# Staging of weight casts, two moved weight loads and a last loop without GpSimd arithmetic, in an eight-core Trainium2 kernel

## The reference

```python
xn = layernorm(x)
mixed_q = xn @ Wq + bq ; mixed_k = xn @ Wk + bk
q_w = softmax((mixed_q @ Wqa + bqa) / 8, over the rows)      # 16 heads
pooled_q = sum over rows of q_w * mixed_q                     # one vector of 1024
mixed_qk = mixed_k * pooled_q
k_w = softmax((mixed_qk @ Wka + bka) / 8, over the rows)
pooled_k = sum over rows of k_w * mixed_qk
s = (pooled_k * mixed_q) @ Wt + bt + mixed_q
y = relu(xn @ W_fc.T)**2 @ W_proj.T                           # hidden width 4096
spikes = five steps of a threshold recurrence on y, their mean
out = x + s * silu(spikes)
```

## Time and profile before

| what | us |
|---|---|
| the timed runs | 1747.59 and 1940.24, median 1843.92 |
| the profiled execution | 1742.46 |
| its span on the slowest core (core 7) | 1740.9 |
| spans of the 8 cores | 1725.4 to 1740.9 |
| TensorE matmul busy | 1333.2 (77% of the span) |
| DVE, ACT, POOL busy | 706.6, 382.5, 228.6 |

### The profile page before, as it was taken

The page is one execution under the profiler, slowest core; times in us unless marked ns, Lnnn a source line. Parts: engine busy times, 40 slices in busy tenths (PEclk is TensorE's granted clock), DMA queues, the critical chain, the costliest instruction groups (busy, mean ns, idle before and its releaser), DMA issues.

```text
span 1740.9 us, 26823 instructions; the slowest of 8 cores (1725.4 to 1740.9 us)
## 1 busy us (share of the span) xinstructions
PE 1333.2 (77%) x8997; PEld 833.0 (48%) x8997; DVE 706.6 (41%) x1297; ACT 382.5 (22%) x828; POOL 228.6 (13%) x308
## 2 busy tenths in 40 slices
PE   0001999999999999999999999999931460558884
PEld 0000666666666666666666666666620130223332
DVE  3222435545546455465464553653432211322221
ACT  1332221322313213223122132231210101021111
POOL 1332000000000000000000000000000102035454
PEclk9999999999999999999999999999965755779997
DMA  5996101111011011110110111101075219147774
GB/s 162 290 295 210 62 13 62 43 44 55 32 62 56 20 61 43 44 56 31 62 56 25 56 43 44 44 25 43 26 225 165 84 30 297 55 137 232 224 230 162
DMA packets 59648, 170.00 MB, mean 98 GB/s; under 512 B 9415, under 2 KB 9815, under 8 KB 59498
## 3 DMA queue, kind: packets, MB, share of 16 engines
q1 hardware_dynamic: 34810, 86.29, 16.8%
q0 software_dynamic: 24704, 82.00, 13.5%
HBM read 117.80 MB, written 50.46 MB: 97 GB/s over the span
## 4 chain that ended last, share of the span: by engine, by line
PE 67%; DMA 15%; DVE 6%; ACT 4%; issue 4%; POOL 2%; SPq 2%; DVEq 0%; ACTq 0%; POOLq 0%
PE PS L481 26%; PE PS L460 24%; PE PS L375 6%; DMA AM<-cnt_scratch 3%; DMA OB<-WfcT 3%; DMA OB<-WprojT 3%; PE PS L854 3%; PE PS L625 2%; POOL OB L883 2%; PE PS L379 2%; DVE YS L877 2%; PE PS L760 2%; DMA OB<-Wk 1%; ACT YS L490 1%; DMA AB<-xn_scratch 1%
## 5 line engine op out<-in xcount | busy, mean ns | idle before, releaser
L481 PE MATMUL PS<-AB,AM 128*128 128x512 bf16 x2048 | 533.5, 380 | 15.5 <-ACT YS L490 13.8
L460 PE MATMUL PS<-SCA,AB 128*128 128x256 bf16 x4096 | 530.3, 273 | 0.0
L460 PEld LDWEIGHTS PS<-SCA,AB 128*128 128x128 bf16 x4096 | 400.5, 98 | 153.2
L469 DVE TENSOR_TENSOR AM<-RB 128x256 bf16<-128x256 f32 x512 | 217.1, 424 | 481.5 <-PE PS L481 283.3
L465 ACT ACTIVATE RB<-PS 128x256 f32<-128x256 f32 x512 | 196.7, 384 | 793.6 <-PE PS L460 327.9
L481 PEld LDWEIGHTS PS<-AB,AM 128*128 128x128 bf16 x2048 | 186.6, 98 | 172.6 <-issue 31.4
L375 PE MATMUL PS<-SCA,AM 128*128 128x256 bf16 x1024 | 137.2, 277 | 139.7 <-DVE SCA L383 116.9
L375 PEld LDWEIGHTS PS<-SCA,AM 128*128 128x128 bf16 x1024 | 100.6, 99 | 155.5 <-issue 142.9
L515 DVE SCALAR_TENSOR_TENSOR AM<-YS,AM 128x1024 bf16<-128x1024 f32 x128 | 156.0, 1219 | 0.8
L854 PE MATMUL PS<-AM,AB 128*128 128x512 bf16 x384 | 95.1, 397 | 37.0 <-issue 21.7
L519 POOL DMA_DIRECT2D cnt_scratch<-AM x32 | 20.6, 645 | 756.2 <-DVE AM L469 419.6
(11 more groups left out here) (107 smaller groups left out, 773.7 us busy)
## 6 DMA issues: line engine op xcount, KB each, us to landing
XF<-x SPq DMA_DIRECT2D x64, 512.0 KB, 4.5
out<-OB POOLq DMA_DIRECT2D x32, 512.0 KB, 6.3
xn_scratch<-SCA POOLq DMA_DIRECT2D x16, 512.0 KB, 3.6
xtm_scratch<-SCA POOLq DMA_DIRECT2D x32, 256.0 KB, 4.9
OB<-WfcT POOLq DMA_DIRECT2D x32, 256.0 KB, 6.3
YS<-WfcT SPq DMA_DIRECT2D x32, 256.0 KB, 6.5
YS<-WprojT SPq DMA_DIRECT2D x32, 256.0 KB, 5.6
OB<-WprojT POOLq DMA_DIRECT2D x32, 256.0 KB, 5.6
```

The lines of the kernel that those rows point to most:

```text
L460: pl.comp("tensor", lambda te, hb=hb, lt=lt, rh=rh, c=c: te.matmul(hb[:, 0:256], lt, rh, start=(c == 0), stop=(c == 7)), reads=a1keys(c * ...
L469: pl.comp("vector", lambda v, h2=h2, rr=rr: v.tensor_mul(h2, rr, rr), reads=[krr], writes=[("h2", g3)])
L481: pl.comp("tensor", lambda te, yb=yb, lt=lt, rh=rh, j=j: te.matmul(yb[:], lt, rh, start=(j == 0), stop=(j == 31)), reads=[kh2] + a2keys(j ...
```

## The change

1. `cast_nslots` starts at 4 and is never set to 8. The slots 2 and 6 of the list, used in the four-slot rotation, are now loaded by SyncE's queue (they hold ACT's pieces); 0 and 4 stay with GpSimd. All staging lies in OB.
2. The small casts of Wqa and Wka move from the end of startup to just behind Wq.
3. The load of the q scores is issued before the 32+12 loads of the transition, hence before the barrier. Three groups of `patch_total` go.
4. 16 pieces of Wt are cast into AM right behind those of WkT. The casts of Wt behind the pooling of k stay as well, so Wt is loaded and cast twice.
5. Wk is cast into AB2[24576:32768] and read from there. The mixed_q blocks 8 to 11 that lay there are loaded behind the pooling of k.
6. All 16 loads of mixed_q go from SyncE's queue to GpSimd's: 8 ahead of the Wk casts, 8 behind the pooling of k and ahead of the Wt casts.
7. Last loop: silu into two buffers of YS in turn, the DVE products straight into OB, and the add of x as a DVE instruction in place on OB. GpSimd only issues the stores.

```diff
-            ("gpsimd", "lw4", OB[:, 512:1024], ("stg", 0)),
-            ("sync", "lw5", YS[:, 512:1024], ("ys", 0)),
+            ("sync", "lw5", OB[:, 512:1024], ("stg", 0)),
+            ("gpsimd", "lw4", YS[:, 512:1024], ("ys", 0)),
...
-            ("gpsimd", "lw6", OB[:, 1536:2048], ("stg", 1)),
-            ("sync", "lw7", YS[:, 1536:2048], ("ys", 1)),
+            ("sync", "lw7", OB[:, 1536:2048], ("stg", 1)),
+            ("gpsimd", "lw6", YS[:, 1536:2048], ("ys", 1)),
-        cast_nslots = [8]
+        cast_nslots = [4]
...
-            for wsrc, dst, nm in ((Wqa_d, WA, "WA"), (Wka_d, WB, "WB")):
...
             cast_flush()
-            cast_nslots[0] = 4
-
-        cast_nslots[0] = 8
         for d in range(8):
             cast(Wq_d[...], AM[...], [("WSM", d)])
+        for wsrc, dst, nm in ((Wqa_d, WA, "WA"), (Wka_d, WB, "WB")):
+            for d in range(8):
+                cast(wsrc[d * 128:(d + 1) * 128, :], dst[:, d * 16:(d + 1) * 16], [(nm, d)])
...
+        pl.dma("sync", "lqs", lambda s: s.dma_start(SC1, qs_d.ap()),
+               reads=[("qsd", b) for b in range(NB)],
+               writes=[("SC1",), ("xnb", 0), ("xnb", 1)])
         for g in range(NT3):
...
         for d in range(8):
             cast(WkT_d[...], AB2[:, d * 1024:(d + 1) * 1024], a2keys(d * 1024, 1024))
+        for d in range(8):
+            cast(Wt_d[d * 128:(d + 1) * 128, :], AM[:, d * 1024:(d + 1) * 1024], [("WSM", d)])
...
-        for bb in range(12):
-            pl.dma("sync", f"lmq{bb % 2}", ... AB2 <- mq_d[bb])
+        for bb in range(8):
+            pl.dma("gpsimd", f"lmq{bb % 2}", ... AB2 <- mq_d[bb])
...
-            cast(Wk_d[...], AM[:, d * 1024:(d + 1) * 1024], [("WSM", d)])
+            cast(Wk_d[...], AB2[:, 24576 + d * 1024: 24576 + (d + 1) * 1024],
+                 a2keys(24576 + d * 1024, 1024))
...
-        for bb in range(12, NB):
-            pl.dma("sync", f"lmq{bb % 2}", ... SCA <- mq_d[bb])
+        for bb in range(8, NB):          # 8 to 11 into AB2, 12 to 15 into SCA
+            pl.dma("gpsimd", f"lmq{bb % 2}", ...)
         for d in range(8):
             cast(Wt_d[d * 128:(d + 1) * 128, :], AM[:, d * 1024:(d + 1) * 1024], [("WSM", d)])
...
-                YS[:, 1024:2048], cslot, AF.Silu, scale=0.2),
-                reads=[("cntr", t % 2)], writes=[("g3",), ("pqrow",)])
-            sg = YS[:, 0:1024]
+                gbuf, cslot, AF.Silu, scale=0.2),     # gbuf: half t % 2 of YS
+                reads=[("cntr", t % 2)], writes=[("g3", t % 2), galias])
+            ot = OB[:, (t % 2) * 1024:(t % 2 + 1) * 1024]
...
+                        v.tensor_mul(ot[:, nh * 512:(nh + 1) * 512], bank[:],
+                                     gbuf[:, nh * 512:(nh + 1) * 512]),
...
-            pl.comp("gpsimd", lambda g, ot=ot, xt=xt, sg=sg: g.tensor_add(ot, sg, xt),
-                    reads=[("sg3",), ("xf3", t % 3)], writes=[("ob3", t % 2)])
+            pl.comp("vector", lambda v, ot=ot, xt=xt: v.tensor_add(ot, ot, xt),
+                    reads=[("xf3", t % 3), ("ob3", t % 2)], writes=[("ob3", t % 2)])
```

More of the change, by code:

```diff
@@ L436, in build_nc @@
                  [("WSM", d)])
+        for wsrc, dst, nm in ((Wqa_d, WA, "WA"), (Wka_d, WB, "WB")):
+            for d in range(8):
+                cast(wsrc[d * 128:(d + 1) * 128, :], dst[:, d * 16:(d + 1) * 16],
+                     [(nm, d)])
         cast_flush()
@@ L577, in build_nc @@
                    reads=[("xtmd", g)], writes=a1keys(g * 1024, 1024))
[L578 to L581, removed]
         for i in range(12):
@@ L586, in build_nc @@
                    reads=[("xnd", i)], writes=a2keys(8192 + i * 2048, 2048))
[L587 to L590, removed]
         pl.barrier()
@@ L644, in pool_phase @@
                 for nh in range(2):
[L645 removed]
+                    rh = wrhs_ap[:, wrhs_col + dc * 1024 + nh * 512: wrhs_col + dc * 1024 + nh * 512 + 512]
                     pl.comp("tensor", lambda te, lt=lt, rh=rh, dc=dc, nh=nh: te.matmul(
@@ L671, in row_to_fm @@
                     reads=[("ps", 7)], writes=[(dstname, c_) for c_ in range(CH)])
[L673 to L677, removed]
         pool_phase("q", SC1, [("SC1",)], SC2, [("SC2",), ("xtb", 0), ("xtb", 1)],
-                   0, [("WSM", d) for d in range(8)])
+                   AM, 0, [("WSM", d) for d in range(8)])
         PQROW = YS[0:1, 1024:2048]
@@ L694, in build_nc @@
                  a2keys(d * 1024, 1024))
+        for d in range(8):
+            cast(Wt_d[d * 128:(d + 1) * 128, :], AM[:, d * 1024:(d + 1) * 1024],
+                 [("WSM", d)])
         cast_flush()
@@ L768, in build_nc @@
                 p0_xnload(b + 2, extra=[("SC1",)])
-        for bb in range(12):
+        for bb in range(8):
             base = 8192 + bb * 2048
-            pl.dma("sync", f"lmq{bb % 2}",
-                   lambda s, bb=bb, base=base: s.dma_start(
+            pl.dma("gpsimd", f"lmq{bb % 2}",
+                   lambda g, bb=bb, base=base: g.dma_start(
                        AB2[:, base: base + 2048], mq_d[bb]),
@@ L780, in build_nc @@
         for d in range(8):
-            cast(Wk_d[d * 128:(d + 1) * 128, :], AM[:, d * 1024:(d + 1) * 1024],
-                 [("WSM", d)])
+            cast(Wk_d[d * 128:(d + 1) * 128, :],
+                 AB2[:, 24576 + d * 1024: 24576 + (d + 1) * 1024],
+                 a2keys(24576 + d * 1024, 1024))
         cast_flush()
         pool_phase("k", SC2, [("SC2k", b) for b in range(NB)], SC1,
-                   [("SC1e",), ("SC1",), ("xnb", 0), ("xnb", 1)], 0,
-                   [("WSM", d) for d in range(8)])
+                   [("SC1e",), ("SC1",), ("xnb", 0), ("xnb", 1)], AB2, 24576,
+                   a2keys(24576, 8192))
         PKROW = YS[0:1, 0:1024]
@@ L804, in build_nc @@
                         15: [("xtb", 1)] + [("SC2k", b_) for b_ in range(8, 16)]}
-        for bb in range(12, NB):
[L806 to L817, removed]
+        for bb in range(8, NB):
+            if bb < 12:
+                base = 8192 + bb * 2048
+                dst, wkeys = AB2[:, base: base + 2048], a2keys(base, 2048)
+            else:
+                dst = SCA[:, (bb - 12) * 2048:(bb - 11) * 2048]
+                wkeys = MQ_SLOT_KEYS[bb]
+            pl.dma("gpsimd", f"lmq{bb % 2}",
+                   lambda g, bb=bb, dst=dst: g.dma_start(dst, mq_d[bb]),
+                   reads=[("mqd", bb)], writes=wkeys)
         for d in range(8):
```

21 lines of the change are left out of this document (10 added, 11 removed).

## The result

| | us |
|---|---|
| before, median of 10 executions | 1744.1 |
| after, median of 11 | 1826.3 |
| ratio after to before, 95% interval | 1.048 (1.046 to 1.050) |
| profiled execution of after, its span on core 1 | 1825.7, 1824.1 |
| predicted | 1773 (1745 to 1800) |

The change makes the kernel slower by 4.8%, outside the range. (The medians hold a few disturbed executions of both kernels; ratios are of undisturbed ones.) The page's slices of after, PE and GB/s, against the earlier trace rows: TensorE idles for five slices of 45.6 us where it did for three, and startup moves 182 to 193 GB/s (slices three to five).

The account below looks back on a forecast made before the run. Transfers bound startup and transition, TensorE the main stage, waits for counts the last loop. 34.4 + 0 + 15.5 - 12.6 + 10.2 - 16.6 = +30.9 on 1742.5 gave 1773 us, range 1745 to 1800.

Parts of the forecast that it names:

- Part 1: Startup through four slots: 35 large cycles of 4.4 us and 4 small of 3.3, L383 at 203.2 for 168.8, +34.4 us.
- the late pair: WkT's last casts in before: counting them gives 17.39 us over 3.5 cycles, 5.0 each, used only as upper bound.
- The second queue: Startup: half the pieces on SyncE bring the cycle to 4.4 us, from 4.45 (WkT) and 4.67 (Wt) on GpSimd alone.
- My upper cycle of 5.0: Startup's upper bound for a slot's cycle, read from WkT's casts in before; it made the startup term +55.4 us.
- Rival B: Startup and later casts: the slot cycle is 5.0 because late pairs come in startup too; +58 us, 1800; chance 0.20.
- Part 4: Wt casts behind WkT: seven more cycles of 4.4 us ahead of the scaling of WB, +15.5 us.
- Parts 5 and 6, Wk: Wk casts take 17.7 us for 30.3, as mixed_q loads no longer come out just before them; -12.6 us.
- mixed_q and Wt: Behind the pooling of k: eight mixed_q loads on GpSimd's queue delay the even Wt pieces behind them; +10.2 us.
- Part 7: Last loop: two-tile loop over the counts shortens, 5.45 us a tile for 5.94; with the first tiles, -16.6 us.
- the 2.4 of the first tiles: Start of the last loop: an add 1.1 us shorter, twice, saves 2.4 us; included in the last loop's -16.6.
- Rival D: Last loop reaches TensorE's own pace, 4.54 us a tile; +4.5 us, 1747; needs count landings under about 4.2; chance 0.08.
- Parts 2 and 3: Early Wqa gives nothing beyond cycles already counted; q scores loaded before the barrier leave softmax near 1324, 0 (-3 to +1).

Follow-up runs that it names:

- e2: Changed kernel with all four staging slots on GpSimd's queue; 1808.0 us, 1.036 of before.
- e3: Changed kernel with all four staging slots on SyncE's queue; 1768.1 us, 1.013 of before.
- e5: Changed kernel with both pieces of a pair on one queue, one pair on GpSimd's and the other on SyncE's; 1814.3 us, 1.040 of before.
- e11: Changed kernel with own planner keys for each slot and each destination half, so DVE's and ACT's casts are free of one another; 1812.7 us, 1.041 of before.
- e12: Changed kernel with all casts on SyncE's queue and only two staging slots in startup; 1870.6 us, one execution.
- e6: Changed kernel without the early Wt casts behind WkT; 1805.1 us, 1.035 of before.
- e7: Changed kernel with the load of mixed_q block 13 no longer waiting for that of block 12; 1824.2 us, 1.046 of before.
- e4: Kernel before with only the changed last loop; 1722.9 us, 0.988 of before.
- e1: Changed kernel with eight staging slots again in startup and four behind it; 1751.8 us, 1.004 of before.

## Why the prediction was wrong

**Part 1, the step that failed.** The form of the sum was right, 35 large cycles behind each other; its cycle of 4.4 was not. Put the mean cycle of after on core 1, 5.55, into the same sum and it gives 33.5 + 35 x 5.55 + 4 x 3.3 + 2.5 = 243.5, against 242.4 in the trace. Of the 39 us that the term missed, some 25 are already there with all four slots on GpSimd's queue, the arrangement of the rows (e2, L383 228 for the forecast 203, cycle 5.1); the second queue adds another 12 (240), and core 1 is 2 above the median. Three choices made it 4.4:

- *The landing.* 3.3 is the median for WkT on core 7 in before. Its eight cores give 3.3 to 3.9 for WkT and 3.5 to 4.0 for Wt; I had read one core, and it was the lowest. In steady state, in startup, it is 3.8 (e2, 3.6 to 4.1 by the core) and 3.9 (e3).
- *The cycle that the rows gave.* I threw the late pair out of the value and kept it only as a bound. With it the row gave 5.0, and one GpSimd queue measures 5.1 (e2). On e2's slowest core, where the median is 5.4, the cycles spread from 4.4 to 6.5 (first and last tenth): late pairs come throughout, and not only in that burst.
- *The second queue*, which I took as a gain of 0.05 to 0.27. It is a loss of 0.4 (5.5 against 5.1) and of 12 us of L383 (240 against 228). What the runs show: the landing is 4.4 (4.2 to 4.8 by the core) with a pair over two queues and its casts in a fixed order, 3.8 on GpSimd's queue alone (e2), 4.0 with each pair on one queue (e5) and 4.2 with two queues and free casts (e11). That the two pieces slow each other because they leave 0.23 us apart is argued from the timeline and fits e5 and e11; it is not measured alone. A move of both to SyncE was never a term of my sum, and is worth 35 us (240 to 205) to after.

The Trainium skill says in DMA: Bandwidth & Descriptors, section "Rules for kernel authors", that spreading transfers over the issuing engines doesn't help bandwidth and only saves issue time. The runs agree and go further: 1826 over two queues, 1768 over SyncE's alone. The Trainium skill's law for GpSimd's path (same page, section "Anatomy of one DMA — SWDGE (gpsimd) path"), 2.0 us and bytes over 436 GB/s, is an estimate of 2.6 for a piece. With four in flight GpSimd's queue measures 3.8 (e2), SyncE's 3.9 (e3); only two in flight come near it, 2.8, and that run is on SyncE's queue (e12).

**The bounds.** My upper cycle of 5.0 gave +55; +73.6 came. A bound from a burst of 14 casts behind prefetched ones is no bound for a steady state that no row showed. The sensitivity was there, 45 us per us of cycle, and e3 to after spans 4.7 to 5.5: a range of 55 us held about 1.2 us of cycle, and I had put most of the chance within 0.35 of a value taken at its low end.

**Rival B** had the right direction with too small a size: it was given 0.20 and 1800. Its late pairs and its cycle of 5.0 are what one GpSimd queue shows (5.1, e2). The loss by the second queue was in no rival.

**Part 4** is the same error: +21.8 for 15.5. The 39.5 us less 2.5 are seven cycles of 5.3, and seven times 0.9 above 4.4 are the missing 6.3. e6 confirms that the stage waits for these casts.

**Parts 5 and 6, Wk**: right, -13.0 for -12.6. **mixed_q and Wt**: +14.1 for +10.2. That the loads delay the pieces behind them was right (e7); the wait of block 13 for block 12 I had overlooked, and its price alone is 2; the other 2 stay open. Whether GpSimd's even pieces are held by its queue or by the load on the engines was not told apart: no run moved the even pieces alone.

**Part 7**: right in total, by two errors that offset each other. From tile 2 to tile 31 it is -18.0 for a forecast of -14.2 (5.32 us a tile for 5.45), and the 2.4 of the first tiles did not come (+0.8). Alone the part gives -20.7 (e4). The counts are still what ACT waits for, 134.4 us in 28 waits from 1640 on, and DMA moves 236 GB/s at 0.72. But there DVE's products wait for ACT only 11 times (30.6 us) and for TensorE 18 times (53.8 us), so the loop over the counts, which my sum took as the limit, is not shown to be the only one. Rival D's TensorE pace was not reached; the landing of the counts is 6.2.

**Parts 2 and 3**: nothing from the early Wqa, as said: L383 holds TensorE. The main stage and transition cost 4.1, of 0 forecast. 1.9 of these are here, PE's timeline of after at the restart:

```profile
249.32 1.89 PE L375 MATMUL PS<-SCA,AM 128*128 128x256 bf16 x8
...
251.43 1.05 PE L375 MATMUL PS<-SCA,AM 128*128 128x256 bf16 x8
```

On this core four groups of eight products take 1.87 to 1.89 before the pace is 1.05; on core 7 of before it was two. Two more at 0.84, with their bias products, are 1.9. Over all cores it takes two to four groups in both kernels, so this is a difference between the two cores compared and not a cost of the change. The granted clock reads 1.00, the upper of its two levels, there in both, right after the idle stretch; why the first products are slow is not shown. After:

```profile
243.00:251.00 8.00, 8.00 (x35) 4.31 (x34) 1.58 (x4) 0.15 (x1) 0.00 (x0) 1.00 0.00 1
```

A further 1.7 lie between the last relu work and the softmax, across the load burst (1274.62 to 1323.74 in before, 1350.68 to 1401.48 in after). Of these, 1.2 are the later start of the loads behind that of the q scores: the 32 loads begin at 1350.41, 0.3 before the last relu work, where the 29 of before began 1.5 before it. The burst itself is 2.8 longer and the softmax starts 2.3 sooner behind its end, much as forecast. The last half of a microsecond lies in the main stage.

**Slips in the working.** "3.3 to land a piece less its own transfer" is 3.3 - 0.9 = 2.4 and not 1.7, which would make the mixed_q term +10.9. The casts of WkT take 17.7 and not 16. An add that is 1.1 shorter twice is 2.2 and not 2.4. And this kernel's time tells less than 2% from no change: the ratio came with 0.2% either side.

## What to carry to other kernels

Staging slots are transfers in flight: before halving them, price the cycle as landing at that depth, cast and re-issue, with rows from all cores. If the only rows are of a short burst, take the burst's worst cycle as the value and go above it for the bound. In this kernel SyncE's queue closed the loop sooner than GpSimd's, and two queues that issued a pair together were worse than either alone. In a tight loop over few buffers a fifth of a microsecond counts (here 9 us over 45 cycles): count the cycles first, then set the range and the chances by them.

## What the runs showed of the hardware

- Landing of 256 KB with all eight cores loading: 2.8 with two in flight and 3.9 with four on SyncE's queue (e12, e3), 6.0 with eight over two queues (e1). DMA share on the slowest core, 100 to 150 us: 0.51, 0.73, 0.97, at 143, 224 and 286 GB/s. The first of these:

```profile
100.00:150.00 50.00, 0.00 (x0) 0.00 (x0) 5.98 (x14) 8.03 (x13) 0.00 (x0) 1.00 0.51 143
```

- From the end of a cast to the re-issue that waits for it: 0.07 us on SyncE (e3, after), 0.55 on GpSimd (e2, after). The issue then takes 0.33 on SyncE and 0.55 on GpSimd.
- The same four slots and casts give L383 at 205, 228, 228 or 240 by the assignment to queues alone.
- The first products after the idle startup took 1.8 times their time (1.89 for 1.05) for two to four groups of eight, by the core, after 115 to 120 us of idling (before) and after 184 to 188 (after) alike. The granted clock read 1.00 meanwhile.
